# Expert stage of a two-layer transformer kernel: the untested part of the tokens as one batch, and one weight transfer per expert

## The reference, cut to what matters

```python
E_R, E_Z = (32, 8); K = 6; SCALE = 2.5
scores = softmax(x @ classifier_weight.T)
_, topk_idx = top_k(scores + e_score_correction_bias[None, :], K)
topk_w = take_along_axis(scores, topk_idx, axis=1) * SCALE
w_full = zeros((T, 40)).at[arange(T)[:, None], topk_idx].add(topk_w)
out0 = x * w_full[:, E_R:].sum(axis=-1, keepdims=True)
def body(out, xs):
    Wgu, Wd, we = xs
    gate, up = jnp.split(x @ Wgu.T, 2, axis=-1)
    y = jax.nn.silu(gate) * up @ Wd.T
    return (out + we[:, None] * y, None)
```

## Time and profile before

| | |
|---|---|
| median of 3 runs | 1077.02 us (1076.58 to 1079.13) |
| the profiled execution | 1073.0 us |
| its span in the trace | 1071.4 us |
| TensorE matmul busy | 932.7 us, 87% of the span |
| TensorE weight loads busy | 724.8 us, 68% |
| VectorE busy | 698.3 us, 65% |
| ScalarE busy | 414.2 us, 39% |
| GpSimd busy | 136.7 us, 13% |
| DMA | 87.07 MB, mean 81 GB/s |

### The profile page before, as it was taken

How to read it: one execution, slowest core, us unless ns; L and a number is a source line. 1 busy time by engine, 2 the same in 40 slices (tenths; PEclk the granted TensorE clock), 3 DMA queues, 4 the chain that set the end, 5 groups by cost and what they waited for, 6 DMA issues and landing times.

```text
span 1071.4 us, 20769 instructions
## 1 busy us (share of the span) xinstructions
PE 932.7 (87%) x7430; PEld 724.8 (68%) x7430; DVE 698.3 (65%) x1518; ACT 414.2 (39%) x970; POOL 136.7 (13%) x129
## 2 busy tenths in 40 slices
PE   2996899999989679999998845799999987898987
PEld 1663687788857349898997734577777765455554
DVE  4445577777735805455554464688888885899995
ACT  1342566666645551111111113366665664112211
POOL 7012000000001430000000004000000001344442
PEclk8998899999986989999999979799999998999999
DMA  9688444455032650202112304544544300000000
GB/s 283 179 219 193 94 89 96 100 100 92 17 105 77 172 166 16 76 16 61 31 42 82 107 14 105 108 89 91 99 92 88 77 3 1 5 9 13 13 13 17
DMA packets 129487, 87.07 MB, mean 81 GB/s; under 512 B 52194, under 2 KB 129122, under 8 KB 129378
## 3 DMA queue, kind: packets, MB, share of 16 engines
q1 hardware_dynamic: 129378, 85.58, 34.3%
HBM read 67.52 MB, written 17.79 MB: 80 GB/s over the span
## 4 chain that ended last, share of the span: by engine, by line
issue 32%; PE 28%; DVE 27%; DMA 7%; SPq 2%; POOL 2%; ACT 1%; POOLq 0%; DVEq 0%; ACTq 0%
PE ps L794 12%; DVE ext L1219 8%; PE ps L801 6%; DMA qscr<-qsp 3%; DVE Pr L1167 2%; DVE Pr L1172 2%; DVE Pr L1170 2%; PE ps L651 2%; DMA wgu<-wgu 1%; PE ps L700 1%; DVE amh L1399 1%; DVE Pr L1421 1%; POOL ksp L492 1%; PE ps L561 1%; DMA Qz<-mT 1%
## 5 line engine op out<-in xcount | busy, mean ns | idle before, releaser
L1219 DVE TENSOR_REDUCE ext<-ps 112x2 f32<-112x750 f32 x256 | 235.3, 932 | 57.0 <-PE ps L623 54.7
L986 ACT ACTIVATE Pr<-ps 125x448 f32<-125x448 f32 x384 | 199.1, 542 | 101.7 <-PE ps L637 88.5
L794 PE MATMUL ps<-xT,wgu 128*128 128x224 f32 x704 | 150.7, 357 | 12.9 <-issue 5.1
L794 PEld LDWEIGHTS ps<-xT,wgu 128*128 128x128 f32 x704 | 133.1, 191 | 23.7 <-issue 13.4
L637 PE MATMUL ps<-Qz,Kp 98*125 98x224 f16 x768 | 131.8, 267 | 16.6 <-DMA Qz<-mT 14.2
L623 PE MATMUL ps<-Kp,Qz 96*112 96x375 f16 x512 | 124.5, 335 | 13.1 <-DMA Qz<-qscr 11.9
L637 PEld LDWEIGHTS ps<-Qz,Kp 98*125 98x125 f16 x768 | 95.8, 139 | 50.0 <-DMA Qz<-mT 18.8
L691 PE MATMUL ps<-wv,ctx 128*125 128x256 f32 x384 | 121.2, 400 | 0.5 <-ACT Vx L992 0.4
L561 PE MATMUL ps<-ctx,wk 128*128 128x375 f32 x256 | 96.8, 527 | 27.5 <-DMA bqk<-bqk 13.3
L1337 DVE TENSOR_TENSOR Pr<-Pr,ps 128x224 f32<-128x224 f32 x88 | 34.2, 388 | 129.9 <-ACT Pr L1057 72.5
L873 PE MATMUL ps<-Pr 128*112 128x352 f32 x256 | 83.8, 472 | 16.9 <-DVE Pr L1421 16.5
(11 more groups left out here) (139 smaller groups left out, 1097.7 us busy)
## 6 DMA issues: line engine op xcount, KB each, us to landing
ctx<-ctxT SPq DMA_DIRECT2D x64, 375.0 KB, 3.9
Kp<-kscr SPq DMA_DIRECT2D x96, 187.5 KB, 4.1
kscr<-ksp SPq DMA_DIRECT2D x32, 375.0 KB, 4.6
wgu<-wgu SPq DMA_DIRECT2D x32, 256.0 KB, 2.8
Qz<-qscr SPq DMA_DIRECT2D x192, 28.0 KB, 4.0
wdn<-wdn SPq DMA_DIRECT2D x32, 128.0 KB, 2.9
qscr<-qsp SPq DMA_DIRECT2D x32, 112.0 KB, 3.8
X<-x_in SPq DMA_DIRECT2D x1, 1792.0 KB, 10.6
```

The lines of the kernel that those rows point to most:

```text
L794: last = mm(ps[:, bank, half_ * CT:(half_ + 1) * CT], wgu_sb[e % NE][:, q, EI * half_:EI * half_ + EI], xT2[:, q, c * CT:(c + 1) * CT], st ...
L986: A(Pr[g % 2][0:KC, j, GI * t:GI * t + GI, :].rearrange("r h q -> r (h q)"), ps[0:KC, 4 + k % 2, 0:GI * S], ACT.Exp, scale=scale).then_inc ...
L1219: V.tensor_reduce(ext[0:S, 2 * p:2 * p + 2], ps[0:S, 2 * (p % 2):2 * (p % 2) + 2, 0:M], AX_X, red).then_inc(row_maximum_taken, 1)
```

## The change

The pieces are listed in `PIECES`: batch 0 alone, then (1,2), (3,4) ... (13,14), then batch 15 alone, nine in all. The untested first piece is batch 0 of 112 tokens. The rest has eight pieces, seven of two batches and one of one. The mask is made of batches 1 to 15. Gate and up weights and down weights of an expert lie behind each other in DRAM, rearranged on the host so that each of the 128 partitions takes one row of 3 KB, and are loaded in one transfer with one semaphore. The wait of `first_down` for the down weights is gone; `first_gate_up` waits for the whole.

```diff
-CH = 8
-CB = B // CH
-CT = CB * S
+PIECES = [(0, 1)] + [(b, min(2, B - b)) for b in range(1, B, 2)]
+CH = len(PIECES)
+CT = 2 * S
...
-        wgu_sb = [sb(f"wgu{p}", [128, C2, 2 * EI]) for p in range(NE)]
-        wdn_sb = [sb(f"wdn{p}", [128, D]) for p in range(NE)]
+        expert_sb = [sb(f"expert{p}", [128, C2 * 2 * EI + D]) for p in range(NE)]
...
                     def load_expert(e):
-                        sp.dma_start(wgu_sb[e % NE][:, :, :], wgu[e].rearrange("(c p) o -> p c o", p=128)).then_inc(
-                            gate_up_weights_loaded[e % NE], 16)
-                        sp.dma_start(wdn_sb[e % NE][:, :], wdn[e]).then_inc(down_weights_loaded[e % NE], 16)
+                        sp.dma_start(expert_sb[e % NE][:, :], wexp[e]).then_inc(expert_loaded[e % NE], 16)
...
                     def gate_up(e, c, bank, done):
+                        b, nb = PIECES[c]
                         for half_ in (0, 1):
                             for q in range(C2):
-                                last = mm(ps[:, bank, half_ * CT:(half_ + 1) * CT],
-                                          wgu_sb[e % NE][:, q, EI * half_:EI * half_ + EI],
-                                          xT2[:, q, c * CT:(c + 1) * CT], start=(q == 0), stop=(q == C2 - 1))
+                                last = mm(ps[:, bank, half_ * CT:half_ * CT + nb * S],
+                                          expert_sb[e % NE][:, EI * (2 * q + half_):EI * (2 * q + half_ + 1)],
+                                          xT2[:, q, b * S:(b + nb) * S], start=(q == 0), stop=(q == C2 - 1))
                         last.then_inc(done, 1)
...
-                    def down(e, h, bank, done):
-                        for v in range(CB):
-                            last = mm(ps[0:S, bank, v * D:(v + 1) * D], h[:, v * S:(v + 1) * S], wdn_sb[e % NE][:, :],
+                    def down(e, c, h, bank, done):
+                        for v in range(PIECES[c][1]):
+                            last = mm(ps[0:S, bank, v * D:(v + 1) * D], h[:, v * S:(v + 1) * S], expert_sb[e % NE][:, C2 * 2 * EI:],
                                       start=True, stop=True)
...
                     def first_gate_up(e):
...
-                            pe.wait_ge(gate_up_weights_loaded[e % NE], 16 * (e // NE + 1))
+                            pe.wait_ge(expert_loaded[e % NE], 16 * (e // NE + 1))
...
                     def first_down(e):
...
-                        pe.wait_ge(down_weights_loaded[e % NE], 16 * (e // NE + 1))
...
-                            A(hfirst[e % 2], ps[:, e % 2, 0:CT], ACT.Silu).then_inc(first_silu_ready, 1)
+                            A(hfirst[e % 2][:, 0:S], ps[:, e % 2, 0:S], ACT.Silu).then_inc(first_silu_ready, 1)
...
-                    ch.link(V.tensor_reduce(used[0:S, :], W[0:S, CB * ET:].rearrange("q (b e) -> q e b", e=ET)[:, 0:ER, :],
+                    ch.link(V.tensor_reduce(used[0:S, :], W[0:S, ET:].rearrange("q (b e) -> q e b", e=ET)[:, 0:ER, :],
...
-                        for v in range(CB):
-                            b = CB * c + v
+                        for v in range(PIECES[c][1]):
+                            b = PIECES[c][0] + v
```

More of the change, by code:

```diff
@@ L94, in step, with build @@
         self.eng.reg_add(self.reg, self.reg, n)
-def build(nc, x, ctxT, attn, wc, ebias, powers, wgu, wdn, fg, fu, fd, out):
+def build(nc, x, ctxT, attn, wc, ebias, powers, wexp, fg, fu, fd, out):
     ctx = ExitStack()
@@ L175, in build @@
         hT = spare1[:, 3 * FI + D + C2 * S:3 * FI + D + (C2 + 6) * S].rearrange("p (c q) -> p c q", c=6)
-        kfull = [spare1[:, CH * CT + C2 * M * n:CH * CT + C2 * M * (n + 1)].rearrange("p (c m) -> p c m", c=C2)
+        kfull = [spare1[:, 8 * CT + C2 * M * n:8 * CT + C2 * M * (n + 1)].rearrange("p (c m) -> p c m", c=C2)
                  for n in (0, 1)]
@@ L241, in build @@
         router_exps_ready = sem("router_exps_ready")
-        gate_up_weights_loaded = [sem(f"gate_up_weights_loaded{p}") for p in range(NE)]
-        down_weights_loaded = [sem(f"down_weights_loaded{p}") for p in range(NE)]
+        expert_loaded = [sem(f"expert_loaded{p}") for p in range(NE)]
         used_by_token = sem("used_by_token")
@@ L818, in first_down @@
                             pe.wait_ge(first_added, e - 1)
-                        down(e, hfirst[e % 2], 4 + e % 2, first_down_ready)
+                        down(e, 0, hfirst[e % 2], 4 + e % 2, first_down_ready)
                     def rest_gate_up(e, c):
@@ L829, in rest_down @@
                         pe.wait_ge(rest_added, n)
-                        down(e, hrest[c % 2], 6 + c % 2, rest_down_ready)
+                        down(e, c, hrest[c % 2], 6 + c % 2, rest_down_ready)
                     first_gate_up(0)
@@ L1061, in rest_silu @@
                         act.wait_ge(rest_gate_up_ready, rest_n.now())
-                        A(hrest[c % 2], ps[:, 2 + c % 2, 0:CT], ACT.Silu).then_inc(rest_silu_ready, 1)
+                        n = PIECES[c][1] * S
+                        A(hrest[c % 2][:, 0:n], ps[:, 2 + c % 2, 0:n], ACT.Silu).then_inc(rest_silu_ready, 1)
                     first_silu(0)
@@ L1334, in _, with gate @@
                     rest_gates, rest_adds = Tally(dve, "dve_rest_gates"), Tally(dve, "dve_rest_adds")
-                    def gate(h, bank, done):
-                        V.tensor_tensor(h, h, ps[:, bank, CT:2 * CT], ALU.mult).then_inc(done, 1)
+                    def gate(c, h, bank, done):
+                        h = h[:, 0:PIECES[c][1] * S]
+                        V.tensor_tensor(h, h, ps[:, bank, CT:CT + PIECES[c][1] * S], ALU.mult).then_inc(done, 1)
                     def add(e, c, bank, done):
-                        for v in range(CB):
-                            b = CB * c + v
+                        for v in range(PIECES[c][1]):
+                            b = PIECES[c][0] + v
                             xb = X[:, b * D:(b + 1) * D]
@@ L1349, in first_gate @@
                             dve.wait_ge(first_silu_ready, e + 1)
-                            gate(hfirst[e % 2], e % 2, first_gated)
+                            gate(0, hfirst[e % 2], e % 2, first_gated)
                     def first_add(e):
@@ L1360, in rest_gate @@
                         dve.wait_ge(rest_silu_ready, rest_gates.now())
-                        gate(hrest[c % 2], 2 + c % 2, rest_gated)
+                        gate(c, hrest[c % 2], 2 + c % 2, rest_gated)
                     def rest_add(e, c):
@@ L1473, in give, with by_rows @@
         return nc.dram_tensor(name, a.shape, mybir.dt.from_np(a.dtype), kind="ExternalInput").ap()
+    def by_rows(a):
+        n, c, o = a.shape[0], a.shape[1] // 128, a.shape[2]
+        return a.reshape(n, c, 128, o).transpose(0, 2, 1, 3).reshape(n, 128, c * o)
     g = {k: np.asarray(v) for k, v in inputs.items()}
@@ L1486 @@
             give("powers", 2.0 ** np.arange(ER // 2, dtype=np.float32).reshape(1, -1)),
-            give("wgu", g["L0_ffn_gate_up_proj"][:ER].transpose(0, 2, 1)),
-            give("wdn", g["L0_ffn_down_proj"].transpose(0, 2, 1)),
+            give("wexp", np.concatenate([by_rows(g["L0_ffn_gate_up_proj"][:ER].transpose(0, 2, 1)),
+                                         by_rows(g["L0_ffn_down_proj"].transpose(0, 2, 1))], axis=2)),
             give("fg", g["L1_ffn_w_gate"]), give("fu", g["L1_ffn_w_up"]), give("fd", g["L1_ffn_w_down"])]
```

## The result

The changed kernel takes 1095.98 us (median of 4 runs, 1093.61 to 1101.51) against 1076.8 us before: a ratio of 1.0182, 95% interval 1.0146 to 1.0219. It is slower, and 2.3 us from the forecast of 1093.7. The profiled execution took 1093.61 us (span 1091.8).

A forecast was written before the change was run, and what follows sets the result against it. Long runs of skipped experts were taken as bound by fetching TensorE's own code. Terms -0.4 + 2.0 - 0.4 - 0.45 + 15.2 - 1.0 + 1.7 = +16.7 on 1077.0 gave 1093.7 us, range 1083 to 1102.

The forecast's parts named there:

- start, to the mark of expert 2: Expert 1's shorter gate-up at the stage's start saves 0.7 us, against its own +0.28: sum -0.4.
- half clock in experts 7 and 22: TensorE's clock may fall in long skip runs, so the next used expert begins at 1.2 GHz: 0 to 3.5, taken +1.7 us.
- runs 3 to 6 and 16 to 21: Long runs of skipped experts, paced by code fetching: only the ends move, -0.2 us for each run.
- expert 10's stretch (9 to 11): Three skips of 8.09 us become skip, used expert (19.30), skip, 23.3 us together: +15.2 us.
- transfer: Expert weights in one 384 KB issue instead of two: late only at third steps of runs, 0 to +1; taken 0.
- B: Rival: the used set stays at 8, so no cost for expert 10; 1078.3 us, 64 rest SiLUs; chance 0.05.
- A: Rival: skips follow their matmuls and loads, not code fetching; faster, 1065 to 1075, say 1070 us; chance 0.08.
- C: Rival: instruction packets queue behind 3 KB rows, lengthening fetches in long runs by 0.5 us each; 1100 us; chance 0.07.
- a used expert over 20 us: Named sign that the forecast is wrong, meaning a piece not hidden; used experts were expected 19.3 us apart.
- S: Later theory, from the experiments: code is fetched block by block in order, skipped or not, at so much time per byte.
- One instruction packet per skip: Expert stage: each skip's jump passes a rest body of over 200 instructions and needs a fetch of 16 KB.
- A lone skip: I take 2.0: A single skip between used experts takes between its matmuls, 1.32 us, and expert 13's 3.04; taken 2.0.

The follow-up runs named there:

- e4: Kernel before with only the weight transfer changed, one of 384 KB in 3 KB rows with one semaphore: 1074.18 us, ratio 1.0001.
- e1: Changed kernel without run-time tests in the expert loop, used experts written into the program, nothing jumped over: 1067.64 us, ratio 0.9938 to the kernel before.
- e3: Changed kernel with the mask made of batches 2 to 15 only, so expert 10 is skipped again: 1081.14 us, ratio 1.0073 to the kernel before.
- e6: Changed kernel with one more 512-column matmul ahead of the first gate-up in a skipped expert's branch: 1108.04 us, ratio 1.0309 to the kernel before.
- e7: Kernel before with rest pieces 2 to 7 in a TensorE loop of three trips, tests and jumps kept: 1060.44 us, ratio 0.9875.
- e9: Changed kernel with weights in two transfers of 1 KB rows and two waits, as before: 1094.1 us, ratio 1.0202 to the kernel before.
- e5: Changed kernel run once more, unaltered, as partner on the same chip: 1091.22 us, ratio 1.0173 to the kernel before.
- e12: Kernel before with 15 never-executed matmuls (60 instructions) more in the rest body of each of the 24 skipped experts: 1091.39 us, ratio 1.0186.
- e10: Changed kernel with ten never-executed matmuls (40 instructions) more in expert 0's rest body: 1100.31 us, ratio 1.0234 to the kernel before.
- e11: Changed kernel with 22 never-executed matmuls (88 instructions) more in expert 0's rest body: 1103.3 us, ratio 1.0275 to the kernel before.

## Why the prediction was right, and where not

The changed kernel's marks against those of before, by the terms of the sum (us):

| term | predicted | measured |
|---|---|---|
| start, to the mark of expert 2 | -0.4 | +2.0 |
| seven used experts, matmuls | +2.0 | +1.75 |
| half clock in experts 7 and 22 | +1.7 | +3.6 |
| runs 3 to 6 and 16 to 21 | -0.4 | +1.25 and +1.1 |
| tail 23 to 31 | -0.45 | +1.15 |
| expert 10's stretch (9 to 11) | +15.2 | +13.8 |
| expert 13 | -1.0 | -1.7 |
| transfer | 0 | 0 (e4: 1.0001) |
| stage | +16.7 | +22.9 |
| outside the stage | 0 | -2.5 |

**Right in its mechanism.** The count of 72, expert 10 as the largest term, a used expert of 19.26 (19.30 predicted), the skips of a run held up by code rather than by matmuls or loads, the clock falling in the runs, and nothing for the transfer: each stands in the profile, and e1, e3, e4, e6, e7 and e9 show them one by one. B falls by the 72 SiLUs. A falls for this kernel by the 13.9 us of "issue", and is true of the kernel without branches (e1). C falls by e4 and e9: 3 KB rows change nothing. The time came out nearer than the terms deserve, which is luck: the stage was 6 us more than summed; the span's gain was 20.4 and the median's 19.2, and 2.5 us came off elsewhere. That is over the 2 us that I had named as a sign of error. It looks like scatter: what follows the stage took 447.6 us in the kernel before, 449.6 in e4, 445.1 and 444.8 in the two profiles of the changed kernel, and 444.5 to 450.4 over all profiles. Another named sign came true as well, "a used expert over 20 us": 1, 7 and 22 took 20.32, 21.36 and 20.74. Its cause is the clock (0.95, 0.90 and 0.93 over these stretches, with TensorE busy throughout), not a piece that shows. And marks in the runs stood up to 4.48 us apart, not 3.1 to 3.6.

**"If code fetching sets the pace, halving the matmuls moves nothing but the ends"** failed. It left out that the change makes the code longer: a ninth piece, 253 instructions for 239. By S the 58.6 us of the three runs grow by 5.9%, 3.4 us; measured 62.1 - 58.6 = 3.5. That near a match is luck: the same runs took 57.6 us in e4 with the pieces of before, and 60.7 (e5) and 61.2 (e9) with the new ones, so the growth is some 2 to 4.5 us. e12 shows the same pace at another size: 70.8 us for 299 instructions. The matmuls saved in the first skip of a run (1.31 for 2.38) are given back at once: the next skip takes 3.4 to 3.5 for 2.38. Whether the half clock in the runs adds to it was not separated.

**"One instruction packet per skip: each jump lands where nothing is loaded"** gave the right rate from the wrong rule. There is a packet per skip because an expert's code happens to be about one block. The trace of before gave a hint: 29 packets for a stage whose code is some 30 blocks, though 24 of 32 rest bodies are jumped over. Of the Trainium skill's two statements quoted in the prediction, the second (2048 instructions of memory, so that the jump would stay inside) finds no support in e7, e10 or e12. The first (a taken branch waits for its target) is compatible, but e12 adds that a block that lies whole between is fetched too.

**"A lone skip: I take 2.0"** was between two true values. It is 1.31 where no block's end falls into it and about 3 where one does (e6, e10, e11). The long stay in a used expert does not help then: in e10 and e11 skips stall right behind 19 us of it, though the prediction had their code fetched in that time. In this kernel all of 9, 11, 13 and 16 are free, worth 1.4 us at expert 10 and 0.7 at 13.

**"With half the columns it ends some 1.4 us earlier"**, the start: expert 1's gate-up, 3.30 us in the earlier trace rows, takes 4.35 here, because 2.17 us of "issue" stand in its middle. The matmuls are shorter as predicted; expert 0's skip became a code stall, where I had counted it as bound by its matmuls; and expert 1's own step grew by 1.15 us, 0.9 more than its matmuls. But that last part is not the change's: e4, with the pieces of before, has 20.37 us for expert 1 at a clock of 0.94, where the first profile of before had full clock from its mark on and 19.18.

**The clock**: 2.1 and 1.5 us for experts 7 and 22, 3.6 for 1.7, at the upper bound of 3.5. In the second profile of the same kernel (e5) it is 1.0 and 1.05, 2.0 in all, near the forecast, so the term scatters by almost its own size. The mechanism is shown by e6.

**The transfer**: "only at the third step of a run ... can it be late, 0 to +1". It was (445.93, 1.95 us; three times, 5.6 us in all), and as predicted it took the place of a wait for code.

## What to carry to other kernels

A branch that skips a long unrolled body is not free: the body's code is fetched whether or not it is executed, here at 3.2 to 3.3 us per 16 KB, and work shortened below that pace brings nothing. Compare the instruction packets of a stage with the size of its code, and put the long side of a branch into a loop (e7: -1.25%, the same matmuls) before making the short side cheaper. Before an untested part is shrunk, count which cases newly fall under the test: three tokens here brought in a whole expert, 1.1% of the time.

## What the runs showed of the hardware that was not expected

- Code that no run executes set the time: 60 instructions more in each skipped body cost 1.86% (e12), and 40 or 88 instructions once, ahead of the stage's skips, made the changed kernel 0.5% (not clear of noise) and 0.9% slower (e10, e11), with stalls of 1.1 to 2.7 us at other lone skips.
- Instruction packets per stage were 17, 29, 31 and 34 for codes of 17.9, 29.9, 31.6 and 35.5 blocks: the fetch goes over jumped code too, in e12 over two blocks of which no instruction runs (6 packets more in the program for 5.6 blocks more of code, where it would be 4 without them).
- Four instructions more per expert (257 for 253; 256 for 252 without labels) put a stall at the same matmul of every skip, and a mean skip from 3.00 to 3.66 us (e6), although the code is only 1.6% longer. The extra matmul of 0.85 us is in that as well. The 0.3 us per skip by which the steps in its runs (3.8 to 4.3) exceed those of the changed kernel are not explained by S. Whether the matmul's own time or the place of the cut makes them was not separated.
